# Two global attentions: the mask moved from TensorE into VectorE's maximum, and the weightings of two steps run together

## What is computed

```python
att = jnp.einsum('bsgmd,btgd->bgmst', q, k) / scale          # first
att = jnp.where(causal, -jnp.inf, att)
att = jax.nn.softmax(att, axis=-1)
ctx = jnp.einsum('bgmst,btgd->bsgmd', att, v)
...
scores = jnp.einsum('bqhd,bkhd->bhqk', q, k) * scale          # second
scores = jnp.where(allowed[None, None], scores, jnp.finfo(scores.dtype).min)
attn = jax.nn.softmax(scores, axis=-1)
out = jnp.einsum('bhqk,bkhd->bqhd', attn, v)
```

## Time and profile before

| what | value |
|---|---|
| median of three runs | 5685.35 us |
| the profiled execution's own time | 5680.27 us |
| its span, first to last instruction | 5678.7 us |
| mean granted TensorE clock over the span | 0.836 of 2.4 GHz |
| first exp to last exp of attention B_ | 206.0 to 1208.9 us |
| first exp to last exp of attention G_ | 2630.5 to 3662.4 us |
| share of the span: PE, DVE, ACT, POOL | 81%, 54%, 41%, 21% |

### The profile page before, as it was taken

How to read it: one execution, slowest core, us unless ns; L and a number is a source line. 1 busy time by engine, 2 the same in 40 slices (tenths; PEclk the granted TensorE clock), 3 DMA queues, 4 the chain that set the end, 5 groups by cost and what they waited for, 6 DMA issues and landing times. The chain is left out here.

```text
span 5678.7 us, 81976 instructions
## 1 busy us (share of the span) xinstructions
PE 4580.8 (81%) x25572; PEld 2818.9 (50%) x25572; DVE 3085.3 (54%) x5402; ACT 2347.5 (41%) x4143; POOL 1218.5 (21%) x1612
## 2 busy tenths in 40 slices
PE   4999999962799997458999999757698796779687
PEld 2444434432688786223343334235466674556566
DVE  1677667632344443556676667447565446746444
ACT  1255445540444443112455455513354433345342
POOL 1011111114100001310111101013487002368300
PEclk8699768786899998775797678779899898989888
DMA  7211111122121211343222222033454103345211
GB/s 215 27 29 28 28 27 30 29 86 87 60 78 46 75 47 48 114 127 50 38 41 39 38 39 39 29 120 118 143 156 125 45 22 116 115 154 156 83 33 34
DMA packets 327218, 413.85 MB, mean 73 GB/s; under 512 B 40836, under 2 KB 236289, under 8 KB 323324
## 3 DMA queue, kind: packets, MB, share of 16 engines
q1 hardware_dynamic: 278620, 257.43, 14.5%
q0 software_dynamic: 43680, 148.25, 12.3%
q10 hardware_dynamic: 4608, 4.20, 0.2%
HBM read 252.70 MB, written 156.19 MB: 72 GB/s over the span
## 5 line engine op out<-in xcount | busy, mean ns | idle before, releaser
L509 DVE TENSOR_REDUCE G_mpart<-G_pm 128x1 f32<-128x512 f32 (+3 forms) x1152 | 705.1, 656 | 364.9 <-PE G_pm L419 356.9
L509 DVE TENSOR_REDUCE B_mpart<-B_pm 128x1 f32<-128x512 f32 (+3 forms) x1152 | 704.3, 656 | 324.8 <-PE B_pm L419 316.2
L495 ACT ACTIVATE G_p<-G_psc 128x1024 f32<-128x1024 f32 (+3 forms) x640 | 544.7, 894 | 494.6 <-PE G_psc L458 493.6
L495 ACT ACTIVATE B_p<-B_psc 128x1024 f32<-128x1024 f32 (+3 forms) x640 | 543.5, 894 | 468.2 <-PE B_psc L458 467.4
L419 PE MATMUL G_pm<-G_ks,G_qs 48*128 48x512 f32 (+3 forms) x1280 | 532.0, 531 | 9.0 <-DVE G_mpart L509 4.1
L419 PE MATMUL B_pm<-B_ks,B_qs 48*128 48x512 f32 (+3 forms) x1280 | 522.0, 521 | 8.7 <-DVE B_mpart L509 4.0
L1695 POOL TENSOR_SCALAR J_pr<-J_pr,J_rc 128x256 f32<-128x256 f32 x512 | 462.7, 916 | 41.3 <-DVE J_rc L1833 38.9
L458 PE MATMUL G_psc<-G_qs,G_ks 50*128 50x512 f32 (+3 forms) x1280 | 365.2, 461 | 15.7 <-issue 13.2
L435 PE MATMUL G_po<-G_p,G_v 128*32 128x512 f32 (+3 forms) x2560 | 370.6, 657 | 6.7 <-DVE G_o L523 6.0
L419 PEld LDWEIGHTS G_pm<-G_ks,G_qs 48*128 48x128 f32 x1280 | 235.1, 228 | 270.8 <-DVE G_mpart L509 168.4
L435 PE MATMUL B_po<-B_p,B_v 128*32 128x512 f32 (+3 forms) x2560 | 360.5, 641 | 8.5 <-DVE B_o L523 6.6
(11 more groups left out here) (305 smaller groups left out, 7709.0 us busy)
## 6 DMA issues: line engine op xcount, KB each, us to landing
J_v<-lve SPq DMA_DIRECT2D x64, 520.0 KB, 3.8
J_k<-lkT SPq DMA_DIRECT2D x64, 512.0 KB
lve<-I_v SPq DMA_DIRECT2D x64, 260.0 KB, 2.1
lqT<-I_tT SPq DMA_DIRECT2D x64, 256.0 KB, 2.4
lkT<-I_tT SPq DMA_DIRECT2D x64, 256.0 KB, 2.6
J_q<-lqT SPq DMA_DIRECT2D x64, 256.0 KB
ein<-Z_z SPq DMA_DIRECT2D x8, 1228.0 KB
E_xin<-ein POOLq DMA_DIRECT2D x8, 1152.0 KB
```

Of the source, the lines that this page charges most:

```text
L495: act.activation(p[:, t % 2, 2 * pr:2 * pr + 2, off:CH], psc[:, 2 * pr:2 * pr + 2, off:CH], ACT.Exp, scale=SC).then_inc(e_done[pr], 1)
L509: dve.tensor_reduce(mpart[:, heads[0] % 2, a:a + len(heads), qb, kc], pm[slots[e]][:, 0:len(heads) * w].rearrange("p (h k) -> p h k", k=w) ...
```

## The change

Three edits, all in `attention`.

The mask leaves TensorE. The identity and the matmul L415 are gone; VectorE keeps the mask in a buffer `far` (384 columns of zeros and the 128 of the mask) and for a diagonal piece issues `tensor_tensor_reduce`: scores plus `far`, written back to the bank, with their maximum in `mpart`. It does so once per head, so a piece of two heads takes two. Other pieces keep `tensor_reduce`.

The steps go in twos. TensorE runs the scores of steps t and t+1 with one list entry behind each of the four pairs, then the weightings of steps t-2 and t-1 with nothing between, then the remaining entries. `p` gets four slots (`DEEP`), and exp of step t waits for the weighting of step t-4.

The turn stands 12 pieces behind the end of its chunk instead of 4.

```diff
-        for behind, kind in ((1, "fold"), (4, "turn")):
+        for behind, kind in ((1, "fold"), (12, "turn")):
...
-        p = sb("p", [P, 2, GRP, CH], F32)
+        p = sb("p", [P, DEEP, GRP, CH], F32)
...
-                diag = kc * CH + w == (qb + 1) * P
-                if diag:
-                    pe.matmul(t[:, 0:c * w].rearrange("p (h k) -> p h k", k=w)[:, :, w - P:w], idb[:],
-                              mqk[:].unsqueeze(1).to_broadcast([P, c, P]), start=True, stop=False, skip_group_check=True)
...
+            def score(i, s, t, pr):
+                qc, kb = steps[t]
+                off = max(0, kb - SUB * qc) * P
+                pe.wait_ge(e_done[pr], i * NS + t + 1)
...
             def body(i, s, half):
-                for t, (qc, kb) in enumerate(steps):
...
+                for t in range(0, NS, 2):
...
+                    for n in range(FIRST):
+                        score(i, s, t + n // 2, n % 2)
+                        some(n, n + 1)
+                    for back in (2, 1):
+                        if t:
+                            weigh(i, s, t - back)
+                        elif not static(i, 0):
+                            weigh(i - 1, 1 - s, NS - back)
+                    some(FIRST, len(events))
...
-                        if not static(i, 0) or t >= 2:
-                            act.wait_ge(pv_done, i * NS + t)
+                        if not static(i, 0) or t >= DEEP:
+                            act.wait_ge(pv_done, i * NS + t + 2 - DEEP)
...
+                    if diag:
+                        wait_apart(dve, s_max, k * NP + j + 1, apart)
+                    else:
+                        dve.wait_ge(s_max, k * NP + j + 2)
+                    if diag:
+                        for x, head in enumerate(heads):
+                            last = dve.tensor_tensor_reduce(pm[slots[e]][:, x * w:(x + 1) * w], pm[slots[e]][:, x * w:(x + 1) * w], far[:, CH - w:CH],
+                                                            1.0, -3e38, ALU.add, ALU.max,
+                                                            mpart[:, head % 2, head // 2, qb, kc:kc + 1])
+                        last.then_inc(max_done, 1)
```

More of the change, by code:

```diff
@@ L306, in clear @@
                     for k in range(page, P, page):
-                        last = pool.memset(p[k:k + page, t % 2, :, off:off + k], 0.0)
+                        last = pool.memset(p[k:k + page, t % DEEP, :, off:off + k], 0.0)
                     last.then_inc(cleared, 1)
@@ L420, in event @@
                                      qs[s][rows, qb // SUB, h // 2, qb % SUB * P:(qb % SUB + 1) * P],
-                                     ks[s][rows, h // 2 % NA, kc * CH:kc * CH + w], start=not diag, stop=True,
-                                     skip_group_check=diag)
+                                     ks[s][rows, h // 2 % NA, kc * CH:kc * CH + w], start=True, stop=True)
                 last.then_inc(s_max, 1)
@@ L435, in weigh @@
                     last = pe.matmul(po[VW * h:VW * (h + 1), off:CH], v[s][:, kb, h % nk],
-                                     p[:, t % 2, h, off:CH], start=kb == 0, stop=kb == SUB * (qc + 1) - 1,
+                                     p[:, t % DEEP, h, off:CH], start=kb == 0, stop=kb == SUB * (qc + 1) - 1,
                                      skip_group_check=True)
                 last.then_inc(pv_done, 1)
+            def score(i, s, t, pr):
+                qc, kb = steps[t]
+                off = max(0, kb - SUB * qc) * P
+                pe.wait_ge(e_done[pr], i * NS + t + 1)
+                for h in (2 * pr, 2 * pr + 1):
+                    rows = slice(64 * (h % 2), 64 * (h % 2) + R + 2)
+                    last = pe.matmul(psc[:, h, off:CH], ks[s][rows, h // 2 % NA, kb * P:(kb + 1) * P],
+                                     qs[s][rows, qc, h // 2, off:CH], start=True, stop=True)
+                last.then_inc(s_done, 1)
             def body(i, s, half):
-                for t, (qc, kb) in enumerate(steps):
-                    off = max(0, kb - SUB * qc) * P
-                    events = [(e // NE, e % NE) for e in range(cut[t], cut[t + 1]) if exists(i + e // NE, e % NE)]
+                for t in range(0, NS, 2):
+                    qc, kb = steps[t]
+                    events = [(e // NE, e % NE) for e in range(cut[t], cut[t + 2]) if exists(i + e // NE, e % NE)]
                     if kb == 0:
@@ L472, in _ @@
             all_iterations(pe, body)
-            weigh(NIT - 1, (NIT - 1) % 2, NS - 1)
+            for back in (2, 1):
+                weigh(NIT - 1, (NIT - 1) % 2, NS - back)
         @block.scalar
@@ L531, in body @@
             def body(i, s, half):
-                for t, (qc, kb) in enumerate(steps):
-                    for k, e in spread(i, t):
+                for t in range(0, NS, 2):
+                    qc, kb = steps[t]
+                    events = spread(i, t) + spread(i, t + 1)
+                    for k, e in events[:FIRST]:
                         event(k, e)
@@ L539, in body @@
                             copy_out(i - 1, NC4 - 1)
+                    for k, e in events[FIRST:]:
+                        event(k, e)
             all_iterations(dve, body)
```

28 lines of the change are left out of this document (17 added, 11 removed).

## The result

Four runs of the changed kernel have a median of 6004.82 us (5990.4 to 6014.47), beside 5677.27 us (5664.43 to 5747.86) for the kernel before. The ratio is 1.054, with a 95% interval of 1.047 to 1.062: slower. Ratios leave out those executions of a kernel that were slow at a lower clock, so they aren't quite the quotients of the medians. The profiled execution took 5998.53 us against 5680.27, that is 318 us more; its mean granted clock is 0.791 against 0.836.

A forecast was written before the change was run, and what follows sets the result against it. TensorE's own row of instructions, at two clock levels, was taken as the bound. 123 us (0.45 of the time) and 167 us (0.55) gave 143.8 us per iteration, 266 us more over 16 iterations: 5950 us, range 5670 to 6090.

The forecast's parts named there:

- two waits: In each pair of steps TensorE waits for exp before later scores, and for VectorE to free a bank behind the weightings.
- The chain of a pair at the high clock: Third scores at 1.5 us, fourth 2.45, weightings 3.0 to 4.95; pair 5.6 or 6.4 us long, mean 6.1.
- The switch: Changing between matmuls of 48 or 50 rows and 128: one saved per two steps, 0.2 us, 4 us per iteration.
- Masks on TensorE: Removing 48 mask matmuls per iteration at 0.35 us saves 17 us (10 to 25), which vanishes because TensorE waits instead.
- VectorE's price: The new masked maximum goes at the reduction's rate plus a short second instruction; VectorE works about 100 us per iteration.
- The rival at half the rate: VectorE's new operation runs at half the reduction's rate and VectorE is the bound: 6190 us, chance 0.08.
- The share of the low clock: In the attentions, a fall every three pairs, low for 24 of 43 us: 0.55 of the time against 0.41.
- The formula of two levels: Iteration length from 123 us at the high clock and 167 at the low, weighted 0.45 and 0.55: 143.8 us.
- The granted clock at 0.70 to 0.75: Sign expected in the profile after: this mean clock over the two attentions, with many short stretches.
- The turn and the slots: The turn 12 behind counted as nothing; the four slots of `p` needed by the new order, at no cost.
- Same share: Rival: time at the low clock stays at today's 0.41, 137.9 us per iteration, 5855 us; chance 0.20.
- faster: Rival: back-to-back weightings hold the clock high, low share 0.1, every pair 5.6 us, 5495 us; chance 0.12.

The follow-up runs named there:

- e2: The changed kernel with the masks back on TensorE and the plain reduction on VectorE, steps still in twos: 6161 us, ratio 1.093.
- e7: The changed kernel with exp over only the second half of its columns, the rest of `p` holding ones: 5783 us, ratio 1.026.
- e8: The changed kernel with two list entries behind each of a pair's four scores and none behind the weightings: 5835 us, ratio 1.039.
- e4: The kernel before with the mask of the maximum left out on every engine: 5404 us, ratio 0.956.
- e1: The kernel before with only the mask edit, masks added in VectorE's maximum: 5493 us, ratio 0.970.
- e6: The kernel before with only the turn moved, 12 pieces behind instead of 4: 5666 us, ratio 0.999.
- e10: The kernel before without masks in the maximum, plus four slots of `p` and the turn 12 behind: 5433 us, ratio 0.960.
- e9: The changed kernel with both weightings still back to back, but between the scores of a pair's two steps: 5886 us, ratio 1.042.
- e3: The changed kernel with the weightings apart, that of t-2 behind the scores of t, that of t-1 behind those of t+1: 5583 us, ratio 0.987.
- e5: The changed kernel with an extra 128-row, 512-column matmul ahead of the piece in a pair's first four entries: 6337 us, ratio 1.124.

## Why the prediction was right

The time was 5950 forecast, 6005 measured, inside the range, by the mechanism named: falls of the clock all through the iteration plus two waits. The nearness of the two numbers is in part luck, since terms that were too small and terms that were left out made up for each other. The clearest case: the forecast gave the steps in twos 266 us and the masks' removal nothing, and measured were 499 us for the steps in twos alone (e2 beside its own runs of the kernel before) and 156 us back for the masks. Step by step:

- **The chain of a pair at the high clock: right.** 1.52, 2.43, 3.10 and 5.55 us for 1.5, 2.45, 3.0 and 5.6. Pairs with four entries behind the weightings take 5.72 or 6.84 us, 6.3 on the mean for 6.4, and all nine with pieces 6.04 for 6.1. e7 (222 us) and e8 (170 us) show that both its waits, exp and ring, count, with the clock's share in them.
- **The switch: too dear.** The prediction's own rows give 2 x 0.99 - 1.9 = 0.08 us for a switch saved, not 0.2. Measured is 630.83 - 628.97 = 1.86 us from a double weighting to the next piece, so 0.12 us on that side. It is a term of 4 us per iteration at most and was counted as vanishing.
- **Masks on TensorE: the size right, the place wrong.** A step at the high clock takes 2.45 us in e4 and 2.75 before, so the masks are 40 x 0.30 = 12 us per iteration there, within the 10 to 25 and under the 17 taken. But the prediction let the masks' and switches' gain "vanish, because TensorE waits instead". It did not vanish: e2 and the changed kernel differ by 156 us, nearly the 170 of e1. That TensorE mostly runs at the low clock, where its own work and not the wait sets the pace, would explain it; no run isolates that.
- **VectorE's price: on its scale.** 717 ns at 512 columns are hardly over the 0.7 us named as the limit, and the read is mostly hidden. In the order of before it costs 5.6 us per iteration (e1 beside e4). Some 3 of them show at the high clock, where a step of B_ takes 2.53 us in e1 and 2.45 in e4; where the rest enters is open. The rival at half the rate is refuted by the 717 ns.
- **The share of the low clock: right in direction, 0.62 for 0.55.** The forecast let it fall in every third pair; B_ has 92 falls in 160 pairs, and 35 pairs stay low all through. The forecast took its recurring low stretch, 24 us, from a kernel where weightings stand alone; now low stretches last 8 us and come six times as often.
- **The formula of two levels: the step that was off.** It was "1 / (0.45/123 + 0.55/167)", with the length of an iteration at each level taken as if the same mixture of work ran at both. A clock that swings within a pair sorts the work. Counted by exps, a step at the high clock takes 2.68 us, less than before (2.75), not the predicted 3.08; at the low one 4.91, not 4.18, because the weightings moved there. Both terms were wrong, in opposite directions, and that they nearly cancel is luck. 1 / (0.38/2.68 + 0.62/4.91) = 3.73 us a step is the measured 149 us per iteration over again, against 143.8 forecast: 5 us in each of 16 iterations, 80 us, of which 27 came back outside the attentions.
- **"The granted clock at 0.70 to 0.75":** 0.69, just below.
- **The turn and the slots: nothing**, as forecast (e6, e10).
- **The rivals.** "Same share" is out by the clock; "faster", with the clock held high by denser weightings, is what the runs refute most plainly: grouping them is what brings it down. The clock swings between its levels as the Trainium skill describes it ("TensorE: Matmul & The Clock Gate", on a second failure mode by cycling through PSUM banks), which blames short idle times between groups of matmuls. The trace agrees with this, and doesn't prove it. At the high clock B_ has an idle time of over 0.1 us between matmuls 0.44 times per us after the change, 0.43 in e8 and 0.51 in e9, against 0.21 in e3 and 0.09 before (from the starts and the modelled ends). Grouping the weightings changed both, the stretches without them and the number of short idle times, so neither is excluded. Long idle times are excluded: the longest in B_ after the change is 1.31 us, of the order that the prediction took for its faster case, and the clock fell 92 times all the same.

How much is the clock's? Beside e3, with the same instructions, TensorE is busy for 184 us more in B_ after the change and idle for 37 us more; its wait for exp's `p` has grown by 44. In e9, where most of that wait is gone (11 us), it is 137 and 21 us. So the larger part of the loss, some five sixths, is matmuls that run slower, and the rest is waiting. In points of the whole it is 6.7 from e3 to the changed kernel and 5.5 from e3 to e9; the intervals of the changed kernel and e9 overlap. That grouping the weightings causes it is shown by e3 against e9, which differ in the place of one weighting per pair. What in the grouping lowers the clock stays open: the stretch without 128-row matmuls, or the short idle times that come with it. e5 was meant to tell, and was too costly.

## What to carry to other kernels

Where TensorE alternates dense matmuls with ones of few rows, spread the dense ones evenly, or measure at least: here grouping them saved a switch of some 0.1 us, and about three in four of their matmuls then started at the low clock (0.77, before 0.29). Don't average a two-level clock over a fixed mix of work; ask which work each level will meet. And before moving a mask to another engine, ask whether that value needs it at all: leaving it out of the maximum was worth 4.4%, moving it 3.0%.

## What was not expected of the hardware

- The clock can swing nearly as often as the program's own period: 92 low stretches in 1190 us of B_, in 160 pairs of some 7.4 us, while the same instructions with the weightings apart (e3) had 35. The dense matmuls mostly fall into the low ones.
- A lower idle share doesn't mean a higher clock (e8: 6% idle, clock 0.70; e3: 9%, 0.81), and comes in part from the low clock itself; in the time at the high clock the two idle for 14% and 13%.
- The maximum with an added operand costs hardly more than the reduction alone, 717 against 685 ns at 512 columns, with one operand in PSUM and one in SBUF; the separate read of its result lasts 142 ns, and the next instruction starts with it, not behind it (574.96 us in the timeline above).
